# Score matmuls placed two key blocks ahead instead of one, with a third score buffer, in an attention and FFN kernel on eight cores

## The reference, cut to what matters

```python
q = _feature_map(q, gamma, beta); k = _feature_map(k, gamma, beta)
q = q * D ** (-0.5)
attn = jnp.einsum('bqhd,bkhd->bhqk', q, k) ** 2
attn = jnp.where(mask, attn, 0.0)
o = jnp.einsum('bhqk,bkhd->bqhd', attn, v)
z = jnp.sum(attn, axis=-1)
o = o / (jnp.swapaxes(z, 1, 2)[..., None] + EPS)
```

## Time and profile before

| what | us |
|---|---|
| median of 2 timed runs | 4702.9 |
| lowest and highest | 4689.45, 4716.35 |
| the profiled execution, its own time | 4734.79 |
| its span on the slowest core (core 0) | 4733.2 |
| spans of the other cores | 4669.5 to 4718.9 |

### The profile page before, as it was taken

How to read it: one execution, slowest core, us unless ns; L and a number is a source line. 1 busy time by engine, 2 the same in 40 slices (tenths; PEclk the granted TensorE clock), 3 DMA queues, 4 the chain that set the end, 5 groups by cost and what they waited for, 6 DMA issues and landing times.

```text
span 4733.2 us, 52828 instructions; the slowest of 8 cores (4669.5 to 4733.2 us)
## 1 busy us (share of the span) xinstructions
PE 3056.8 (65%) x13416; PEld 1270.3 (27%) x13416; DVE 1846.3 (39%) x3416; ACT 1814.9 (38%) x2685; POOL 248.5 (5%) x460
## 2 busy tenths in 40 slices
PE   0767767677676723323466577776899999513889
PEld 0333333333333311111111122222343444212334
DVE  0443434435353424554333222122266666333221
ACT  0333332333333212332344455553144444365551
POOL 1000000000000010000000000000000000000000
PEclk9888888888787866656798899998899999855999
DMA  9344343343434363332221211113477667356885
GB/s 181 99 102 121 92 119 102 102 121 95 128 93 115 96 147 108 105 103 77 75 61 51 85 57 57 76 57 98 132 233 237 234 232 233 132 174 211 288 283 196
DMA packets 326545, 628.24 MB, mean 133 GB/s; under 512 B 199792, under 2 KB 207984, under 8 KB 294256
## 3 DMA queue, kind: packets, MB, share of 16 engines
q0 software_dynamic: 65664, 321.94, 23.5%
q1 hardware_dynamic: 260592, 302.92, 21.2%
HBM read 573.34 MB, written 84.93 MB: 139 GB/s over the span
## 4 chain that ended last, share of the span: by engine, by line
PE 25%; DVE 23%; DMA 16%; ACT 13%; issue 10%; SPq 8%; another core or an unknown queue 3%; DVEq 1%; ACTq 1%; POOL 0%; POOLq 0%
SPq L80 8%; PE kv_ps L354 7%; DMA xf<-xfull 5%; PE ops L681 4%; DMA xob<-xown 4%; ACT s2t L664 3%; PE gps L885 3%; DVE s2t L666 2%; PE zps L685 2%; PE sps L653 2%; PE dps L1111 2%; ACT sgn L734 2%; ACT sgn L737 2%; PE ups L897 2%
## 5 line engine op out<-in xcount | busy, mean ns | idle before, releaser
L354 PE MATMUL kv_ps<-wk_sb,xnT 128*128 128x512 bf16 x2560 | 647.3, 420 | 167.2 <-DMA wv_sb<-wvt 87.3
L354 PE MATMUL kv_ps<-wv_sb,xnT 128*128 128x512 bf16 x2048 | 492.2, 405 | 105.6 <-DVE kg L364 105.6
L681 PE MATMUL ops<-s2t,vsb 128*128 128x512 bf16 x768 | 301.3, 392 | 281.9 <-DVE s2t L666 231.7
L666 DVE TENSOR_TENSOR s2t<-s2t,msk_sb 128x512 bf16<-128x512 bf16 x512 | 217.6, 425 | 636.7 <-ACT s2t L664 632.2
L329 PE MATMUL tp_ps<-ident,xnb 128*128 128x128 bf16 x640 | 85.5, 300 | 570.3 <-ACT xnT L335 255.6
L664 ACT ACTIVATE s2t<-sps 128x512 bf16<-128x512 f32 x512 | 305.7, 597 | 331.2 <-PE sps L653 322.0
L354 PEld LDWEIGHTS kv_ps<-wk_sb,xnT 128*128 128x128 bf16 x2560 | 269.0, 106 | 536.5 <-issue 294.9
L885 PE MATMUL gps<-terng,xqs 128*128 128x512 bf16 x1408 | 339.7, 397 | 73.0 <-DVE ternu L753 57.4
L1111 PE MATMUL dps<-dtern,hqts 128*128 128x512 bf16 x1408 | 328.3, 396 | 57.1 <-DMA hqts<-hqtd 53.2
L273 ACT ACTIVATE sgn<-wfp 128x1024 bf16<-128x1024 f32 x264 | 278.9, 1057 | 205.7 <-DMA wfp<-gwt_r 118.7
L653 PE MATMUL sps<-qsb,ksb 128*128 128x512 bf16 x768 | 302.6, 395 | 39.9 <-DMA qsb<-qsc 39.1
(11 more groups left out here) (139 smaller groups left out, 3543.0 us busy)
## 6 DMA issues: line engine op xcount, KB each, us to landing
wfp<-gwt_r POOLq DMA_DIRECT2D x176, 512.0 KB, 5.4
wfpt<-gwt_r POOLq DMA_DIRECT2D x88, 1024.0 KB, 6.5
wfp<-dwt_r POOLq DMA_DIRECT2D x88, 512.0 KB, 4.9
xqs<-xqsc SPq DMA_DIRECT2D x88, 512.0 KB, 4.5
wfpt<-dwt_r POOLq DMA_DIRECT2D x44, 1024.0 KB, 7.7
hqts<-hqtd SPq DMA_DIRECT2D x32, 1408.0 KB, 8.5
xf<-xfull SPq DMA_DIRECT2D x32, 1024.0 KB, 7.8
hgscr<-hgb SPq DMA_DIRECT2D x88, 256.0 KB, 2.5
```

What stands on the lines that cost most here:

```text
L354: TE(lambda e, jj=j, f=fc, w=w_sb: e.matmul(kv_ps[jj][:], xnT[:, f * 128:(f + 1) * 128], w[:, f * DM + jj * 512: f * DM + (jj + 1) * 512], ...
L666: vck = V(lambda e, bb=sb, vv=v: e.tensor_tensor(s2t[bb][:], s2t[bb][:], msk_sb[:, (vv % 16) * 512:((vv % 16) + 1) * 512], ALU.mult), wait ...
L681: TE(lambda e, sl=slot, vv=v, bb=sb, hh=h, n=NC: e.matmul(ops_[hh % 2][:], vsb[sl][:, vv * 128:(vv + 1) * 128], s2t[bb][:], start=(vv == 0 ...
```

## The change

The score matmul of a block is written two blocks ahead instead of one, `sps` and `s2t` get a third buffer each, and the buffer is chosen by v % 3. With it the eight banks of PSUM are in use in this stage: three `sps`, two `ops`, two `zps` and one from the thresholds.

```diff
     s2t = [es_ph3.enter_context(nc.sbuf_tensor(f"s2t{i}", [128, 512], BF16))
-           for i in range(2)]
+           for i in range(3)]
     sps = [es_pp3.enter_context(nc.psum_tensor(f"sps{i}", [128, 512], F32))
-           for i in range(2)]
+           for i in range(3)]
-    sps_free = [("cV", 0), ("cV", 0)]
+    sps_free = [("cV", 0)] * 3
             def emit_S(v):
-                sb = v % 2
+                sb = v % 3
             s_cks = {0: emit_S(0)}
+            if NC > 1:
+                s_cks[1] = emit_S(1)
             for v in range(NC):
-                sb = v % 2
+                sb = v % 3
-                if v + 1 < NC:
-                    s_cks[v + 1] = emit_S(v + 1)
+                if v + 2 < NC:
+                    s_cks[v + 2] = emit_S(v + 2)
```

## The result

| | before | after |
|---|---|---|
| median, us | 4729.68 (10 runs, 4689.45 to 4774.24) | 4514.98 (11 runs, 4487.88 to 4543.93) |
| ratio | | 0.9557 (95% interval 0.9511 to 0.9604) |
| profiled execution, its own time | 4734.79 | 4502.77 |
| span of the slowest core | 4733.2 (core 0) | 4501.2 (core 2) |
| attention there, first score matmul to last O | 940.1 | 722.0 |

The change saves 4.4%, some 210 us by the ratio. A median here can hold executions in which the cores of one half of the chip ran at a lower granted clock and took longer; every ratio is taken without them. Of the 232 us between the two spans, 218 lie in the attention; the other 14 are of the size by which cores and executions of one kernel differ. The median of before is now that of ten runs, the two of before the prediction among them, and lies 27 us above the one that stood there.

A forecast was written before the change was run, and what follows sets the result against it. Bound: a latency ring between engines, two blocks per 2.37 us masked or 1.70 us unmasked. Savings of 83 us (C = 0) and 128 us (C = 1) sum to 211 us, taking 4702.9 to 4492 us; range 4448 to 4550.

The forecast's parts named there:

- The ring and its division by three: Masked blocks: the TensorE, ScalarE, VectorE latency ring of 2.37 us carries three blocks instead of two, 0.79 us each.
- ScalarE as the bound of unmasked blocks: Unmasked blocks: the ring's third, 0.57 us, lies below ScalarE's one Square per 0.69 us, so 0.69 us a block.
- The new wait costs nothing: TensorE: score matmul of block v+2 waits for block v-1's mask multiply or Square, already awaited by earlier ops; priced at nothing.
- The gap at a change of heads stays: Last ops of a head to the next head's first: unchanged, 3.73 us in C = 0, 2.95 us in C = 1.
- The load waits stay: Waits for loads at the attention's start and the switch of query halves: unchanged, 39.1 us together.
- The half clock: C = 0, behind each head's gap: 4.0 us at 1.2 GHz kept whole, losing 1.5 us a head against the new rate.
- The rest of a head of C = 1: Second query half: 1.30 us a head above the sum of its parts, kept unchanged in the forecast 27.14 us.
- ScalarE's wait for the score matmul: Sign in the profile after: this wait in the attention falls from 322 to about 100 us.
- The start: Whole-kernel time before the change, 4702.9 us, the median of two timed runs, from which the saving was subtracted.
- The rival on the clock: Attention after each head's gap: TensorE never regains 2.4 GHz, 1.28 us a block, 137 us more, 4840 us; chance 3%.

The follow-up runs named there:

- filling the gap: Changed kernel plus 8 unread matmuls behind the third score matmul of each head but a half's first: attention 697.9 us, heads 15.69 and 26.70 us.
- across heads with three: Changed kernel with all 768 blocks in one list across heads and halves, score matmul three ahead, four s2t tiles: attention 589.3 us, ratio to before 0.9249.

## Why the prediction was right

It forecast 4492 us and 211 us saved, from 4702.9; the ratio 0.9557 makes it 208 us from the same start. Point by point:

- **The ring and its division by three** (2.37 / 3 = 0.79): 2.36 us with three ops matmuls in it. One ahead with three buffers restored the old time, so the number to divide by is set by the place in the order. Shown.
- **ScalarE as the bound of unmasked blocks** (0.69): ten Squares in a row without a wait. Shown, and shown again where ScalarE set the whole head.
- **The new wait costs nothing**: TensorE's waits have no row of a score matmul that waits for a mask multiply or a Square. Shown. Nor did the kernel with two banks gain, where the score matmul waits for a Square alone; a head of C = 1 came out some 0.3 us longer there, and that much the third bank does bring.
- **The gap at a change of heads stays** (3.73 us, and 2.95 in C = 1): 3.73 and 2.95 us.
- **The load waits stay** (39.1 us): 38.8 us. The loads of a head of C = 1 stayed hidden; no wait for `ksb` or `vsb` stands between heads.
- **The half clock** (1.5 us a head of C = 0): this term was too large. The granted clock of 0.90 over 271.87 us is 54 us at 1.2 GHz, 3.4 us a head for the 4.0 that I kept, and a head of C = 0 took 16.90 us for 17.08, so 1.32 above the ring's 15.58, of which filling the gap gave 1.21 back. The working has a flaw that did little harm: by its own 1.28 us a block, 4.0 us at half clock would have cost a head of before 4.0 x (1 - 1.18 / 1.28) = 0.3 us, not the 1.08 that it puts down to them. In the trace of before the second and third step of a head of C = 0 take 3.01 us together (mean of 15 heads), so the slower matmuls lengthened the ring itself; 1.28 was not its price there.
- **The rest of a head of C = 1**, 1.30 us kept whole: 26.94 for 27.14 us, so 1.10 above the rest of the sum. The prediction named no cause for it. The largest part is a term that its sum had at nothing, the mask multiply that enters the chain at the first masked block, 0.67 us; it is there before and after, so keeping the rest whole was right, by luck rather than by working. Filling the gap gave 0.24 back; 0.2 us stay open.
- **ScalarE's wait for the score matmul**, "about 100 us": 87.8 us.
- **The start**: the prediction took 4702.9 us from two runs. Ten runs of the same kernel give 4729.7. That shifts the forecast up by 27 us; the medians lie 215 us apart for 211 forecast, and the two make the 23 us between 4492 and the median of 4515.0. That the two runs lay low is chance; from their own start the ratio gives 4702.9 x 0.9557 = 4494.6.
- **The rival on the clock**, beside which the prediction put the rule of the Trainium skill (TensorE: Matmul & The Clock Gate, section "A second HAM failure mode: psum-queue depth-cycling"): the granted clock of C = 1 was 0.99 before, 0.98 with a third bank alone, 0.99 with the change, 0.97 two ahead with two banks, and 1.00 across heads with three. The third bank went with 0.01 less in one order and 0.02 more in the other, so the number of banks shows no steady effect. The clock rose where the idle stretches at the changes of heads were filled (0.99 to 1.00, and 0.90 to 0.99 in C = 0) or taken out.

## What to carry to other kernels

When two engines wait for each other in small equal pieces and neither is full, follow one item round and divide the time by the items that are on the way: the place of the producing instruction in its engine's order sets that number, and buffers only allow it. Then look which engine is full next, and move work off it to an engine that has room at that very place, not on average. A gap at a loop's seam costs more than its length when the engine comes out of it at half clock, and one list across the seam removes the gap and nearly all of the half clock (0.98 in C = 0).

## What the runs showed of the hardware that I had not expected

- Eight matmuls that nobody reads, put where TensorE idles at a change of heads, made a head of C = 0 faster by 1.21 us of 16.90, with the granted clock going from 0.90 to 0.99.
- The VectorE reciprocal of 128x512 f32 took 3353 ns, against 692 ns for an add from PSUM of that shape, and 1.41 us for Ln and Exp together on ScalarE as they stand in a row.
